# A feed-forward, attention, feed-forward block on one core: projections in a bank pair of their own, one result bank for the FFN, new orders

## The reference

```python
x = x + 0.5 * ffn(layernorm(x))
x = x + attn(layernorm(x))
x = x + 0.5 * ffn(layernorm(x))

def ffn(x):      # per sequence; H = 512, D = 128
    lt = x[:, 1:17]; even, odd = lt[:, ::2], lt[:, 1::2]
    m1 = (even[:, :4, :, None] * odd[:, :4, None, :]).reshape(B, 512, 128)
    m2 = (even[:, 4:, :, None] * odd[:, 4:, None, :]).reshape(B, 128, 512)
    h = gelu(x @ (W1 + scale * m1).T + b1)
    return h @ (W2 + scale * m2).T + b2

def attn(x):     # 16 heads of 8, linear attention
    q, k, v = x @ Wq.T + bq, x @ Wk.T + bk, x @ Wv.T + bv
    feature(t) = exp((t / sqrt(8)) @ R - 0.5 * sum((t / sqrt(8)) ** 2))
    kv = feature(k).T @ v            # per sequence and head, 8 x 8
    z = 1 / (sum(feature(q)) + 1e-8)
    return (feature(q) @ kv * z) @ Wo.T + bo
```

## Time and profile before

| | |
|---|---|
| median of 2 runs | 171.09 us (170.51 and 171.67) |
| the profiled execution | 170.79 us, of which the span of its instructions is 169.0 us |
| granted TensorE clock | 1.0 over the span |
| busy share of PE, DVE, ACT, POOL | 95%, 81%, 74%, 49% |
| moved by DMA | 19.55 MB, mean 116 GB/s |

### The profile page before, as it was taken

The page is one execution under the profiler, slowest core; times in us unless marked ns, Lnnn a source line. Parts: engine busy times, 40 slices in busy tenths (PEclk is TensorE's granted clock), DMA queues, the critical chain, the costliest instruction groups (busy, mean ns, idle before and its releaser), DMA issues.

```text
span 169.0 us, 3429 instructions
## 1 busy us (share of the span) xinstructions
PE 160.3 (95%) x1052; PEld 141.7 (84%) x1052; DVE 136.8 (81%) x442; ACT 124.3 (74%) x249; POOL 83.5 (49%) x101
## 2 busy tenths in 40 slices
PE   6997999999999999899999998899999999999993
PEld 6975898989798999577988786788997899899893
DVE  1799988899899948989999999999997679943121
ACT  3299958987968497699959768989898575756320
POOL 5345527319814898948972880882760039100000
PEclk9999999999999999999999999999999999999999
DMA  4990417066430144421331161423236616036403
GB/s 107 321 285 7 127 64 186 22 198 160 170 81 4 64 141 169 132 59 50 138 98 30 64 190 67 113 71 105 87 126 206 189 45 186 2 123 192 124 21 103
DMA packets 31409, 19.55 MB, mean 116 GB/s; under 512 B 2608, under 2 KB 28448, under 8 KB 31392
## 3 DMA queue, kind: packets, MB, share of 16 engines
q1 hardware_dynamic: 31104, 19.34, 38.4%
q10 hardware_dynamic: 288, 0.00, 0.1%
HBM read 11.94 MB, written 7.40 MB: 114 GB/s over the span
## 4 chain that ended last, share of the span: by engine, by line
PE 75%; DVE 8%; ACT 7%; issue 5%; DMA 2%; POOL 1%; DVEq 0%; ACTq 0%; POOLq 0%
PE quad L804 33%; PE quad L788 9%; PE quad L789 8%; PE quad L790 8%; PE quad L821 3%; PE quad L823 3%; PE quad L822 3%; PE ps_t L858 3%; ACT xn L480 3%; PE ps_g L839 2%; DMA scale<-in_rows_dram 2%; ACT gl L520 2%; PE ps_g L804 1%; DVE ex L706 1%; PE ps_r L828 1%
## 5 line engine op out<-in xcount | busy, mean ns | idle before, releaser
L804 PEld LDWEIGHTS quad<-w2e,gl 128*128 128x128 f32 x496 | 60.2, 192 | 3.2 <-ACT gl L520 0.4
L804 PE MATMUL quad<-w2e,gl 128*128 128x128 f32 x496 | 60.8, 275 | 0.0
L520 ACT ACTIVATE gl<-quad,cols 128x512 f32<-128x512 f32 x64 | 42.6, 682 | 16.6 <-PE quad L790 15.5
L411 POOL TENSOR_TENSOR rstd<-veps,mhalf 128x4 f32<-128x4 f32 (+1 forms) x16 | 16.6, 1043 | 29.1 <-DVE veps L132 29.0
L788 PE MATMUL quad<-xh,w1h 128*128 128x512 f32 x64 | 28.5, 445 | 0.4 <-ACT gl L520 0.2
L480 ACT ACTIVATE xn<-X,nmr,rstd 128x128 f32<-128x128 f32 x61 | 25.0, 486 | 3.5 <-DVE nmr L592 3.5
L789 PE MATMUL quad<-xl,w1h 128*128 128x512 f32 x64 | 25.2, 394 | 0.0
L790 PE MATMUL quad<-xh,w1l 128*128 128x512 f32 x64 | 25.2, 393 | 0.0
L432 POOL TENSOR_TENSOR X<-X,b2h 128x512 f32<-128x512 f32 x16 | 20.6, 1305 | 1.1 <-issue 1.1
L690 DVE TENSOR_TENSOR X<-quad,X 128x512 f32<-128x512 f32 (+1 forms) x16 | 10.7, 672 | 11.7 <-PE quad L804 11.7
L788 PEld LDWEIGHTS quad<-xh,w1h 128*128 128x128 f32 x64 | 12.2, 190 | 2.9 <-issue 1.2
(11 more groups left out here) (105 smaller groups left out, 281.6 us busy)
## 6 DMA issues: line engine op xcount, KB each, us to landing
ev<-token_rows SPq DMA_DIRECT2D x7, 512.0 KB, 4.1
folded<-tq SPq DMA_DIRECT2D x12, 256.0 KB, 2.0
land<-folded SPq DMA_DIRECT2D x48, 64.0 KB, 2.2
folded<-atq SPq DMA_DIRECT2D x8, 256.0 KB, 2.0
aland<-folded SPq DMA_DIRECT2D x32, 64.0 KB, 2.1
X<-in_x_dram SPq DMA_DIRECT2D x7, 256.0 KB, 5.5
out_dram<-X SPq DMA_DIRECT2D x7, 256.0 KB, 2.6
w1t<-in_w1t_dram SPq DMA_DIRECT2D x1, 256.0 KB, 3.5
```

The source lines that it names most:

```text
L411: pool.tensor_tensor(rstd[:, i, own], veps[:, i, own], mhalf[:, own], ALU.pow).then_inc(s_rstd, 1)
L520: act.activation(gl[:, f % 2, j], ps_h[j % 2], ACT.Gelu, bias=cols[:, j:j + 1]).then_inc(s_gelu, 1)
L804: ins = pe.matmul(y[:, n * P:(n + 1) * P], gl[:, f % 2, j, n * P:(n + 1) * P], w2e[:, f // PER_B % 2, j], start=(j == 0), stop=(j == HB - 1))
```

## The change

- quad keeps four banks, but its last two are now the projections' own pair. Both halves of every chunk use that pair, and qk.a.0 and qk.a.2 wait until the half just before has been read by DVE. ex has four buffers in place of two.
- The FFN has one result bank, ps_y, which was freed by moving gram into columns 0 to 127 of ps_m (mix uses the next two blocks of 128). A down.f.0 waits for the add of chunk f - 1. The last chunk's results go to ps_y, ps_m and ps_r, and are added and stored in three pieces (2, 1 and 1 tiles), the last one issued by ACT.
- The waits that kept attention behind the first FFN and the second FFN behind attention are gone; o no longer shares its wait with the turns. Attention's high and low parts have four buffers in place of five.
- The warm-up is 11 products ahead of lead, in place of 11, 4 and (behind turn.0) 4.
- All five orders are new. TensorE runs the first projections between up.5 and up.6, and up.8 and up.9 among the projections of chunks 6 and 7.

```diff
-WARM_UP = (11, 4, 4)
+WARM_UP = 11
+LAST = [slice(0, 2), slice(2, 3), slice(3, 4)]
-LAND, ALAND, TQ, AH = 3, 2, 2, 5
+LAND, ALAND, TQ, AH = 3, 2, 2, 4
+EX = 4
 "act": (
+        "norm.0 rest.0 first_w1h.0 first_w1h.1 turn.0 norm.1 first_w1h.2 first_w1h.3 norm.2 up.0.0 turn.1 up.0.1 "
+        "load.0 up.0.2 up.0.3 turn.2 norm.3 up.1.0 up.1.1 norm.4 w1h.1 up.1.2 up.1.3 turn.3 up.2.0 up.2.1 norm.5 "
...
+        "anorm.2 anorm.3 up.6.2 up.6.3 aturn.1 feat.0.1 up.7.0 up.7.1 anorm.4 up.7.2 feat.1.0 aturn.2 up.7.3 exp.0.0 "
...
+        "exp.5.1 up.8.0 feat.6.0 gram.5 norm.10 qturn.4 mix.2.1 up.8.1 turn.9 up.8.2 feat.6.1 up.8.3 up.9.0 up.9.1 "
+        "up.9.2 qturn.5 feat.7.0 turn.10 norm.11 norm.12 w1h.5 feat.7.1 up.9.3 exp.6.0 exp.6.1 exp.7.0 exp.7.1 "
+        "up.10.0 up.10.1 turn.11 gram.7 norm.13 qturn.6 mix.3.1 up.10.2 turn.12 up.10.3 up.11.0 up.11.1 qturn.7 w1h.6 "
 "dve": (
...
+        "astats.7 mix.0.0 head_sums.2.1 feat.2.1 amoments.7 o.0 stats.8 moments.8 head_sums.3.0 feat.3.0 z_sums.2 "
+        "norm.8 o.1 z.2 head_sums.3.1 feat.3.1 blocks.8 stats.9 moments.9 head_sums.4.0 feat.4.0 z_sums.3 norm.9 "
+        "mix.1.0 ablocks.7 z.3 head_sums.4.1 feat.4.1 o.2 blocks.9 z_sums.4 head_sums.5.0 odd.4 feat.5.0 w1.4 turn.8 "
+        "w1l.4 head_sums.5.1 feat.5.1 z.4 stats.10 moments.10 o.3 z_sums.5 norm.10 head_sums.6.0 mix.2.0 feat.6.0 z.5 "
+        "blocks.10 stats.11 turn.9 o.4 head_sums.6.1 moments.11 feat.6.1 w2.4 stats.12 norm.11 moments.12 "
+        "head_sums.7.0 feat.7.0 odd.5 turn.10 norm.12 w1.5 blocks.11 blocks.12 w1l.5 o.5 down.8.3 head_sums.7.1 "
 "pe": (
+        "lead.0 select.0 turn.0 select.1 up.0.0 turn.1 up.0.1 up.0.2 up.0.3 turn.2 up.1.0 up.1.1 down.0.0 down.0.1 "
...
+        "qk.0.0 qk.0.1 up.6.0 up.6.1 down.5.0 down.5.1 down.5.2 down.5.3 up.6.2 up.6.3 qk.0.2 qk.0.3 up.7.0 up.7.1 "
+        "down.6.0 up.7.2 qk.1.0 up.7.3 qk.1.1 down.6.1 down.6.2 down.6.3 qk.1.2 qk.1.3 down.7.0 down.7.1 down.7.2 "
+        "qk.2.0 qk.2.1 down.7.3 gram.0 gram.1 qk.2.2 qk.2.3 mix.0.0 qturn.0 mix.0.1 o.0 qk.3.0 qk.3.1 qturn.1 o.1 "
+        "qk.3.2 qk.3.3 gram.2 qk.4.0 qk.4.1 qturn.2 gram.3 mix.1.0 qk.4.2 qk.4.3 mix.1.1 o.2 qk.5.0 qk.5.1 gram.4 "
+        "qturn.3 qk.5.2 qk.5.3 o.3 up.8.0 up.8.1 qk.6.0 qk.6.1 gram.5 qturn.4 mix.2.0 up.8.2 mix.2.1 qk.6.2 qk.6.3 "
+        "o.4 up.8.3 up.9.0 qturn.5 up.9.1 up.9.2 qk.7.0 qk.7.1 down.8.0 down.8.1 up.9.3 down.8.2 qk.7.2 qk.7.3 o.5 "
...
+        "up.15.0 up.15.1 down.14.0 down.14.1 up.15.2 down.14.2 down.14.3 up.15.3 down.15.0 down.15.1 down.15.2 "
+        "down.15.3 "
...
-        ex = sb("ex", [P, 2, 4, P])
+        ex = sb("ex", [P, EX, 4, P])
...
-        ps_y = [quad[:, 2], quad[:, 3]]
-        ps_g, ps_r, ps_m = bank("ps_g"), bank("ps_r"), bank("ps_m")
+        pair = quad[:, 2:4]
+        ps_y, ps_r, ps_m = bank("ps_y"), bank("ps_r"), bank("ps_m")
+        ps_g = ps_m[:, 0:D]
...
+        def y_of(f, n):
+            return [ps_y, ps_y, ps_m, ps_r][n] if f == FC - 1 else ps_y
-        def halves(p, which):
-            return quad[:, 2 * p:2 * p + 2, :].rearrange("p n (k w d) -> p w (n k) d", k=2, w=2)[:, which]
+        def halves(which):
+            return pair.rearrange("p n (k w d) -> p w (n k) d", k=2, w=2)[:, which]
...
+                if stage == "last":
+                    act.wait_ge(s_x3, CHUNKS - 1 + len(LAST))
+                    act.dma_start(chunk_of(out, CHUNKS - 1)[:, LAST[-1]], X[:, CHUNKS - 1, LAST[-1]]).then_inc(s_out, 16)
...
+                    for tiles in LAST if f == FC - 1 else [slice(0, NT)]:
+                        dve.wait_ge(s_d, NT * f + tiles.stop)
+                        dve.tensor_tensor(flat(X[:, to, tiles]), y_of(f, tiles.start)[:, D * tiles.start:D * tiles.stop],
+                                          flat(X[:, to, tiles]), ALU.add).then_inc(s_x1 if f < CHUNKS else s_x3, 1)
...
-                    wait(dve, s_exp, 2 * a + p - 1)
-                    dve.tensor_tensor(heads(ex[:, p]), heads(halves(p, 1)),
+                    wait(dve, s_exp, 2 * a + p - EX + 1)
+                    dve.tensor_tensor(heads(ex[:, (2 * a + p) % EX]), heads(halves(1)),
...
-                    if i == CHUNKS:
-                        pe.wait_ge(s_x2, CHUNKS - 4)
...
-                        if f == CHUNKS:
-                            pe.wait_ge(s_sub, 2 * CHUNKS - 1)
...
-                        if f == CHUNKS:
-                            pe.wait_ge(s_sub, 2 * CHUNKS)
-                        wait(pe, s_x1, min(f - 1, CHUNKS))
-                        wait(pe, s_x3, f - 1 - CHUNKS)
+                        wait(pe, s_x1, min(f, CHUNKS))
+                        wait(pe, s_x3, f - CHUNKS)
+                    if f == FC - 1 and n == 2:
+                        pe.wait_ge(s_x2, CHUNKS)
+                        pe.wait_ge(m_mo, NB)
...
-                            pe.wait_ge(s_gelu, HB * CHUNKS)
+                            pe.wait_ge(s_w1r, LORA)
+                            pe.wait_ge(s_od, 1)
                             pe.wait_ge(k_wal, 1)
-                    if a == 0 and n >= 2:
-                        pe.wait_ge(s_x1, CHUNKS - 1 + n - 2)
                     if n % 2 == 0:
-                        wait(pe, s_sub, 2 * a + n // 2 - 1)
-                    to = quad[:, n]
+                        wait(pe, s_sub, 2 * a + n // 2)
+                    to = pair[:, n % 2]
...
-                        wait(pe, m_gs, i // PER_B)
+                        wait(pe, m_mo, i // PER_B)
```

More of the change, by code:

```diff
@@ L222, in build @@
         ps_h = [quad[:, 0], quad[:, 1]]
-        ps_y = [quad[:, 2], quad[:, 3]]
-        ps_g, ps_r, ps_m = bank("ps_g"), bank("ps_r"), bank("ps_m")
-        picked = [ps_m[:, 0:D], ps_r[:, 0:D], ps_g[:, 0:D], ps_g[:, D:2 * D]]
+        pair = quad[:, 2:4]
+        ps_y, ps_r, ps_m = bank("ps_y"), bank("ps_r"), bank("ps_m")
+        ps_g = ps_m[:, 0:D]
+        picked = [ps_m[:, 0:D], ps_r[:, 0:D], pair[:, 0, 0:D], pair[:, 0, D:2 * D]]
         lead = quad[:, 3]
-        ps_o = [ps_t] * CHUNKS
         ld_x = [sem(f"ld_x{c}") for c in range(CHUNKS)]
@@ L375, in _ @@
                     c = i[0] - CHUNKS
-                    parts = 2 if c == CHUNKS - 1 else 1
-                    for h in range(parts):
-                        tiles = slice(NT // parts * h, NT // parts * (h + 1))
+                    for h, tiles in enumerate(LAST[:-1] if c == CHUNKS - 1 else [slice(0, NT)]):
                         sp.wait_ge(s_x3, c + h + 1)
                         sp.dma_start(chunk_of(out, c)[:, tiles], X[:, c, tiles]).then_inc(s_out, 16)
-            sp.wait_ge(s_out, 16 * (CHUNKS + 1))
+            sp.wait_ge(s_out, 16 * (CHUNKS - 1 + len(LAST)))
         @block.gpsimd
@@ L525, in _ @@
                     wait(act, s_red, 2 * a + p - 1)
-                    act.activation(sq[:, p], halves(p, 0), ACT.Square, scale=0.25).then_inc(s_sq, 1)
+                    act.activation(sq[:, p], halves(0), ACT.Square, scale=0.25).then_inc(s_sq, 1)
                 if stage == "exp":
@@ L543, in _ @@
                     wait(act, s_o, PER_B * b)
-                    act.activation(mo[:], ps_m[:, D:2 * D], ACT.Copy).then_inc(m_mo, 1)
+                    act.activation(mo[:], ps_m[:, 2 * D:3 * D], ACT.Copy).then_inc(m_mo, 1)
                 if stage == "gram" and i % PER_B == PER_B - 1:
@@ L548, in _ @@
                     wait(act, m_kv, b)
-                    act.activation(gs[:], ps_g[:, 0:D], ACT.Copy).then_inc(m_gs, 1)
+                    act.activation(gs[:], ps_g, ACT.Copy).then_inc(m_gs, 1)
         @block.vector
@@ L577, in _ @@
                     dve.wait_ge(k_wv, 1)
-                    dve.tensor_copy(wv2[:], ps_g[:, 0:D]).then_inc(k_wv2, 1)
+                    dve.tensor_copy(wv2[:], ps_g).then_inc(k_wv2, 1)
                 if stage == "stats":
@@ L670, in _ @@
                         dve.wait_ge(s_ev, 16 * i)
-                    even = ps_y[0].rearrange("p (j d) -> p j d", j=LORA) if i == 0 else ev[:, i % 2, LORA:]
+                    even = ps_y[:].rearrange("p (j d) -> p j d", j=LORA) if i == 0 else ev[:, i % 2, LORA:]
                     wait(dve, s_d, NT * PER_B * (i - 1))
@@ L684, in _ @@
                     dve.wait_ge(s_xb, f + 1)
-                    parts = 2 if f == FC - 1 else 1
-                    for h in range(parts):
-                        tiles, part = NT // parts, TOK // parts
-                        dve.wait_ge(s_d, NT * f + tiles * (h + 1))
-                        dve.tensor_tensor(flat(X[:, to, tiles * h:tiles * (h + 1)]),
-                                          (ps_g if h == 1 else ps_y[f % 2])[:, part * h:part * (h + 1)],
-                                          flat(X[:, to, tiles * h:tiles * (h + 1)]), ALU.add).then_inc(
-                            s_x1 if f < CHUNKS else s_x3, 1)
+                    for tiles in LAST if f == FC - 1 else [slice(0, NT)]:
+                        dve.wait_ge(s_d, NT * f + tiles.stop)
```

(31 more changed lines are left out.)

10 lines of the change are left out of this document (6 added, 4 removed), and 94 rows, old and new, of the table ORDER.

## The result

The changed kernel takes 175.24 us (174.65 and 175.82) against 171.09: a ratio of 1.027 (95% interval 1.021 to 1.033), slower. The sign was forecast, but only 2.2 us of the 4.15, and the largest chance, 0.65, stood on less than two per cent either way (up to 174.5). A later series of six runs of the same kernel gave 175.23 against 170.38 (1.0273, 1.0236 to 1.0309).

What follows compares the result with a forecast made beforehand. It took TensorE as 95% busy, with DVE bounding attention; 2.7 (bank pair) + 0.9 (Gelu) + 0.3 (start) - 1.2 (rest) - 0.2 (end) = +2.5 us on 170.8 gave 173.3, range 169.0 to 176.0.

Steps and rivals of the forecast that it cites:

- The bank pair: Attention: each half's projections wait for the half just before, 3.87 us start to start; loss 8.0 against 5.3, +2.7 us.
- the six cycles: Attention, qk.2.2 to qk.5.2: 23.2 us holding 16.5 of work, so 6.7 us lost.
- the 8.0: TensorE's forecast loss in attention, in us: 6.7 from qk.2.2 to qk.5.2 plus 1.3 behind it.
- DVE's queue: Attention from qk.5.2 to gram.7: DVE's list full but not over, 1.3 us lost (0 to 4).
- The signs in the profile: Ex waits at six halves, 6 to 7 us; five table loads; 0.9 us hole before down.15.0; first Gelu near 13.5.
- The rest: Outside start and attention: 2.3 us lost before should shrink by 0 to 2.3; -1.2 taken, the middle.
- What bounds the kernel now: Kernel before: TensorE loses 10.7 us in all; DVE, busy 47.5 of 48 us, bounds attention with in-order chains behind.
- The Gelu ahead of down.15.0: End of the FFN: up.15.3 directly ahead of down.15.0, which needs its Gelu; 0.87 us lost, +0.9.
- The start: Up to up.2.2: shorter warm-up, but ACT's list puts norm.2 and first_w1h before the first Gelu; +0.3 us (-0.6 to +1.2).
- rival 3: Start: shorter warm-up ends just behind the clock's rise; if 1.2 GHz stayed, about 176 us; chance 0.04.
- The last add and store: Kernel end: last add of one tile, 0.28 instead of 0.42 us, ACT's store with none in front; -0.2 us.
- ACT's two more table loads: Gelu and exp alternate: two more loads, 2.6 us of ACT, counted within attention's 1.3 us.

Runs made afterwards that it cites:

- a4_pairs: Changed kernel with a second bank pair, borrowed from the FFN's first product, for halves 3.0, 4.0 and 5.0: 173.50 us (1.0162).
- b2_light: Changed kernel with lighter DVE work: z_sums copies one of each head's eight values instead of summing them: 175.87 us (1.0295).
- c3_before_onepair: Kernel before with both halves of every chunk on one bank pair, orders of mix.2.0, head_sums and feat adapted: 206.85 us (1.2111).
- b4_before_light: Kernel before with z_sums copying one of each head's eight values instead of summing them: 169.66 us (0.9945).
- c1_tail2: Changed kernel with up.15.3 ahead of down.14.2 and down.14.3, and the last chunk's first two tiles in ps_t instead of ps_y: 174.20 us (1.0218).
- a3_tail: Changed kernel with only up.15.3 moved ahead of down.14.2 and down.14.3 in TensorE's list: 175.45 us (1.0282).
- a2_head: Changed kernel with the old precedence in the start: first Gelus ahead of norm.2 on ACT, first_w1l and turn.1 earlier on DVE: 174.73 us (1.0235).
- b1: Changed kernel itself, unedited, run six times beside its variants: median 175.23 us.

## Why the prediction came out as it did

- **The bank pair: right in mechanism, in size with luck.** +2.7 forecast, +3.0 by the stretches. Four of the six cycles came as the chain has them, a4_pairs takes the waits away, b2_light doesn't touch them, c3_before_onepair makes them 16 cycles. But the two parts of the 8.0 missed in opposite ways: counted as the prediction counts, the six cycles lost 24.3 - 16.5 = 7.8 us in place of 6.7, and behind them the profile shows some 0.3 us of idle time up to 118 us in place of the 1.3 that I gave DVE's queue.
- **The signs in the profile: mostly seen.** Five table loads, a hole of 0.94 us ahead of down.15.0, the first Gelu at 13.11 and no cycle under 3.5 us. But the waits for ex are four, not six, and 3.2 us, not 6 to 7, just above the 3 that I had called wrong: part of the loss stands ahead of the o and mix stages, and part of the rest was never idle time (see "The rest").
- **"What bounds the kernel now": mostly wrong.** "DVE bounds attention" was read from 47.5 of 48 us. b4_before_light gives 0.7 us back for 2.7. That the in-order chains named beside it carry the rest is likely, but was not tried.
- **The Gelu ahead of down.15.0: right.** 0.87 forecast from the earlier trace rows, 0.94 measured by starts (read from the chain's rows, as there, it would be 0.78), and c1_tail2 wins 0.8 to 1.0 by removing it. That the same place is the result bank's as well was priced at zero; a3_tail shows that it costs 0.95 as soon as the Gelu is out of the way.
- **The rest: the step that failed.** "I take -1.2, the middle" was an average between two ends with no row for it, and it is 1.5 of the 2.3 us by which the sum fell short. Without the fall of the clock +0.3 was measured between 20 and 70 us and nothing from 118 on. There was hardly anything to shrink: the kernel before is idle for only 0.6 us in those stretches (50 - 49.55 and 47 - 46.83), not 2.3. Most of the 2.3 comes from pricing each 512-column matmul at 0.23 us. The first one behind a stage of another kind stands 0.31 us ahead of the next (11.81 and 12.12 above, then 12.35); the trace of before has 33 such first ones in the two stretches, which makes up to 2.7 us that is no wait and that no new order takes away. The +0.3 is not firm: it is a single wait near 38.5 us, which the three profiled runs with the fall (the first profile, a4_pairs, b2_light) don't have. The first profile of the changed kernel is busy for all of that stretch:

```profile
20.00:70.00 50.00, 50.00 (x336) 45.23 (x335) 41.63 (x145) 42.22 (x83) 31.59 (x36) 1.00 0.35 108
```

- **The start: a term and a rival, both too small.** +0.3 forecast, 0.9 measured without the clock's fall; a2_head, which gave the old precedence back, didn't win it, so that what in the new order costs it stays open. The fall was rival 3, at a chance of 0.04 and with the wrong cause: the clock was up before the warm-up ended (its last two records start at 5.80, lead at 6.03, 0.11 us apart), and it fell afterwards, behind two idle times of about 1 us between few matmuls. It came in 14 of 38 runs with this start, which took 0.6 (b2) to 1.2 us (b1, a3) longer than their neighbours without it. A rule of the Trainium skill (TensorE: Matmul & The Clock Gate, HAM oscillation — how this bites in real kernels) warns of idle gaps that let the clock fall again; this trace agrees with its direction, 0.43 us between starts from 15.7 on, but the gaps that the page means are longer than the 1.2 and 0.9 us here. I had weighed the warm-up instead.
- **The last add and store: -0.2 forecast, -0.35 measured.** From the last matmul's end to the span's end are 2.3 us instead of 2.7.
- **ACT's two more table loads** came (five in all, 1.28 us each, 67.87 and 123.56 among them) and no wait of TensorE stands behind them in the profile; not tried alone.

So 2.5 us became 4.8 in a run without the fall: 1.5 from the rest, 0.6 from the start, 0.3 from attention, less 0.15 at the end.

## What to carry to other kernels

When two buffers become one, time the chain from fill to fill once in the old trace and lay it against what the new order puts between: 3.87 us gave four of six cycles to within 0.1 us, and the other two were longer by what else stood in the way on ACT and DVE. A busy share near 100% doesn't prove a bound; take away a few per cent of that engine's work and look. A loss that comes from a count of matmuls times one price is not yet a wait: look for the waits before you forecast that they shrink. And a term without a row of its own, like a middle between nothing and everything, should widen the range, not move the forecast.
